# Expert slots with the weights as the stationary operand, fetched slot by slot

## What is computed

```python
# layer 0: 16 experts, hidden width 512, each token goes to its 2 best
h = relu(einsum('bsd,edh->bseh', tensor, W1) + b1)
y = einsum('bseh,ehm->bsem', h, W2) + b2
out = einsum('bse,bsem->bsm', gate, y)
# layer 1: 16 experts, hidden width 176, 2 of them a token, and a shared expert z
a = silu(einsum('td,edh->teh', xf, w1) + b1) * (einsum('td,edh->teh', xf, w3) + b3)
y = einsum('teh,ehd,te->td', a, w2, cw) + cw @ b2
```

## Time and profile before

| | us |
|---|---|
| median of 3 runs (548.8 to 549.23) | 548.93 |
| profiled execution, its own time | 548.54 |
| its span, first to last instruction | 546.8 |
| busy: TensorE, VectorE, ScalarE, GpSimd | 440.9, 364.3, 264.4, 250.2 |
| mean granted TensorE clock, as a share of 2.4 GHz | 0.922 |

### The profile page before, as it was taken

The page is one execution under the profiler, slowest core; times in us unless marked ns, Lnnn a source line. Parts: engine busy times, 40 slices in busy tenths (PEclk is TensorE's granted clock), DMA queues, the critical chain, the costliest instruction groups (busy, mean ns, idle before and its releaser), DMA issues.

```text
span 546.8 us, 10536 instructions
## 1 busy us (share of the span) xinstructions
PE 440.9 (81%) x2430; PEld 303.7 (56%) x2430; DVE 364.3 (67%) x1181; ACT 264.4 (48%) x666; POOL 250.2 (46%) x322
## 2 busy tenths in 40 slices
PE   4889733999999992799889889988657779999950
PEld 3667611777777770256555555545524456777730
DVE  6879940355555552679999999999644445656636
ACT  3357610444444430757777678667232115656520
POOL 3105771143444444336348558457549002656560
PEclk9999755899999996989999999999778999999985
DMA  7999874212122604834122500000003020222107
GB/s 240 348 272 247 243 144 81 55 51 55 47 58 55 223 16 127 205 69 96 38 59 70 132 10 21 0 22 21 15 25 99 19 60 22 78 76 79 49 12 231
DMA packets 63420, 51.52 MB, mean 94 GB/s; under 512 B 9180, under 2 KB 54733, under 8 KB 63234
## 3 DMA queue, kind: packets, MB, share of 16 engines
q1 hardware_dynamic: 56434, 40.86, 29.2%
q0 software_dynamic: 5056, 8.48, 4.6%
q10 hardware_dynamic: 1872, 1.52, 1.2%
HBM read 37.19 MB, written 15.60 MB: 97 GB/s over the span
## 4 chain that ended last, share of the span: by engine, by line
PE 46%; DVE 31%; issue 11%; POOL 4%; DMA 4%; ACT 2%; SPq 0%; DVEq 0%; POOLq 0%; ACTq 0%
PE bank L1505 15%; PE bank L1520 8%; PE bank L1597 4%; PE bank L1513 4%; PE bank L1659 4%; DVE qk_sums L1202 4%; POOL sorted_tokens L716 3%; DVE work L1195 3%; DVE big L1195 3%; DVE work L1239 3%; PE bank L1498 2%; PE bank L1551 2%; DVE ln_stats L258 2%; PE bank L1651 2%; PE bank L1627 2%
## 5 line engine op out<-in xcount | busy, mean ns | idle before, releaser
L725 POOL DMA_INDIRECT results<-work x94 | 91.7, 975 | 139.3 <-DVE work L1172 76.3
L1158 DVE TENSOR_TENSOR work<-bank,bias_big 128x512 f32<-128x512 f32 (+1 forms) x94 | 57.1, 608 | 94.0 <-PE bank L1505 92.5
L857 ACT ACTIVATE work<-bank,mcol 128x128 f32<-128x128 f32 x94 | 43.0, 458 | 115.7 <-PE bank L1498 115.7
L1551 PE MATMUL bank<-late,work 128*128 128x512 f32 x192 | 94.6, 621 | 2.4 <-ACT work L873 2.2
L1505 PE MATMUL bank<-big,work 128*128 x188 | 91.4, 568 | 3.6 <-ACT work L857 3.6
L1551 PEld LDWEIGHTS bank<-late,work 128*128 128x128 f32 x192 | 33.9, 195 | 30.6 <-issue 27.0
L1520 PE MATMUL bank<-big,work 128*128 x376 | 49.7, 275 | 0.0
L1520 PEld LDWEIGHTS bank<-big,work 128*128 128x128 f32 x376 | 45.8, 192 | 0.1
L716 POOL DMA_INDIRECT sorted_tokens<-late,router_at x32 | 31.1, 973 | 27.1 <-DVE late L1107 17.6
L766 POOL DMA_INDIRECT sorted_tokens<-rows,router_at x32 | 31.2, 976 | 13.1 <-issue 7.9
L1505 PEld LDWEIGHTS bank<-big,work 128*128 128x128 f32 x188 | 28.8, 194 | 13.1 <-issue 13.1
(11 more groups left out here) (223 smaller groups left out, 984.5 us busy)
## 6 DMA issues: line engine op xcount, KB each, us to landing
work<-sorted_tokens SPq DMA_DIRECT2D x94, 65.0 KB, 1.8
big<-in_w SPq DMA_DIRECT2D x48, 88.0 KB
big<-in_W SPq DMA_DIRECT2D x1, 4096.0 KB
bias_big<-in_b SPq DMA_DIRECT2D x16, 256.0 KB
big<-results SPq DMA_DIRECT2D x16, 256.0 KB, 3.5
sorted_tokens<-zeros SPq DMA_DIRECT2D x2, 975.0 KB
sorted_tokens<-zeros SPq DMA_DIRECT2D x24, 65.0 KB
late<-in_WqkvbT SPq DMA_DIRECT2D x1, 1544.0 KB
```

The costliest lines, as they stand in the source:

```text
L725: pool.indirect_dma_start(ys[l], bass.IndirectOffsetOnAxis(xg[b][:, D:D + 1].bitcast(I32), 0), yo[b], None, bounds_check=TOPK * T - 1, oob ...
L857: act.activation(xgT[b % 2], bank[:, ends[b % 2], 0:P], ACT.Identity, bias=scale_shift[0], scale=scale_shift[1]).then_inc(e_xTc, 1)
L1158: dve.tensor_tensor(hb[b % 2][:, 0:width], bank[:, 1 + b % 2, 0:width], bias_big[:, bass.ds(e * width, width)], ALU.add).then_inc(e_hb, 1)
L1551: last = pe.matmul(bank[:, 2 * k + i, :], h3T[b], Wqkvb[:, k * HD + i * 512:k * HD + (i + 1) * 512], start=True, stop=True)
```

## The change

- Layer 0: the four 128-column blocks of W1 are now the stationary operands and the 128 turned tokens move. The hidden tile comes out with hidden units on partitions, in two banks. The four transposes are gone. The bias is a column (`b1c`): ScalarE does relu with bias on two blocks, VectorE on the other two.
- Layer 1: w1 and w3 are cut in halves of 88 columns, which are stationary (four products). ScalarE does silu with bias out of PSUM on two halves; VectorE does (second product + bias) * silu in one operation for each half. The two transposes and the copy are gone.
- Stages follow closer on each other (lags of TensorE 0, 1, 2 in place of 0, 1, 2, 3 and 0, 1, 3, 4). ScalarE now looks the expert up too.
- W1, w1 and w3 no longer stand in SBUF. A ring of 8 buffers holds the weights of 8 slots. SyncE fetches them for each slot, after its own look-up: one transfer of 256 KB in layer 0, two of 88 KB in layer 1. The first four slots' weights are issued before the wait for the sorted rows, the others among the row loads. `slot_turn` waits for rows and weights together.
- The broadcast bias loads are gone; the biases are loaded as rows, turned by TensorE once and copied by VectorE before the slots of layer 0.

```diff
+        NW, LEAD = 8, 4
+        w1r = [big[:, H0 * b:H0 * (b + 1)] for b in range(NW)]
-            sp.dma_start(W1s.rearrange("p (e h) -> p e h", e=E), W1.rearrange("e d h -> d e h")).then_inc(ld_w0, 16)
...
-                sp.dma_start(bias_big[:, e * H0:(e + 1) * H0], all_row(b1[e, :], H0)).then_inc(ld_w0, 16)
...
+                def load_expert(t):
+                    if t >= NW:
+                        sp.wait_ge(e_h, l * SLOTS + t - NW + 1)
+                    e = bass.ds(experts(t, 1)[0], 1)
+                    if l == 0:
+                        sp.dma_start(w1r[t % NW].rearrange("p (a h) -> p a h", a=1),
+                                     W1[e, :, :].rearrange("e d h -> d e h")).then_inc(e_x[t % NX], 16)
+                    else:
+                        for k, w in enumerate((w1, w3)):
+                            sp.dma_start(w13r[t % NW][:, k * H1:(k + 1) * H1].rearrange("p (a h) -> p a h", a=1),
+                                         w[e, :, :].rearrange("e d h -> d e h")).then_inc(e_x[t % NX], 16)
...
+                for t in range(LEAD):
+                    load_expert(t)
                 rows_written()
-                run_slots(sp, SLOTS, NX, [(0, None), (0, load)], table(mybir.EngineType.SP, tbl, 0, ROWS - P))
+                for s in range(SLOTS + NW):
+                    if s < SLOTS:
+                        load(s, s % NX, s // NX, place(s, 1)[0])
+                    if LEAD <= s < NW:
+                        load_expert(s)
+                    if s >= 2 * NW:
+                        load_expert(s - NW)
...
+            def slot_hidden(t, b, q, e):
+                pe.wait_ge(e_xTc, t + 1)
+                after(pe, e_hTc, t - 1)
+                after(pe, e_hb, t - 1)
                 for c in range(C0):
-                    last = pe.transpose(bank[:, 3 + b % 2, c * P:(c + 1) * P], hb[b % 2][:, c * P:(c + 1) * P], ident[:, :])
+                    last = pe.matmul(hidden_half(b, c), w1r[t % NW][:, c * P:(c + 1) * P], xgT[b % 2],
+                                     start=True, stop=True)
...
             def silu(t, b, q, e):
+                act.wait_ge(e_h, SLOTS + t + 1)
+                after(act, e_act, t - 1)
+                for c in range(2):
+                    last = act.activation(silu1[b % 2][:, c * P:(c + 1) * P], hidden_part(b, 0, c), ACT.Silu,
+                                          bias=b13c[:, 0, bass.ds(e * 2 + c, 1)])
...
             def gated(t, b, q, e):
                 dve.wait_ge(e_silu, t + 1)
+                after(dve, e_o, SLOTS + t - 1)
+                for c in range(2):
+                    last = dve.scalar_tensor_tensor(hbT[b % 2][0:K1, c * P:(c + 1) * P], hidden_part(b, 1, c),
+                                                    b13c[:, 1, bass.ds(e * 2 + c, 1)],
+                                                    silu1[b % 2][:, c * P:(c + 1) * P], ALU.add, ALU.mult)
```

More of the change, by code:

```diff
@@ L217, in build @@
         xgT = [work[:, 2080 + P * b:2080 + P * b + P] for b in range(2)]
-        hb = [work[:, 2336 + H0 * b:2336 + H0 * (b + 1)] for b in range(2)]
         hbT = [work[:, 3360 + H0 * b:3360 + H0 * (b + 1)] for b in range(2)]
-        act1 = [work[:, 4384 + 176 * b:4384 + 176 * b + H1] for b in range(2)]
+        silu1 = [work[0:K1, 2336 + 2 * P * b:2336 + 2 * P * (b + 1)] for b in range(2)]
         sh_at = ob + 12 * D
@@ L526, in uses, with hidden_half, hidden_part, landed @@
             return len(range(b, SLOTS, NX))
+        def hidden_half(b, c):
+            return bank[:, 1 + 2 * (2 * c // C0) + b % 2, (c % (C0 // 2)) * P:(c % (C0 // 2) + 1) * P]
+        def hidden_part(b, k, c):
+            return bank[0:K1, 1 + 2 * k + b % 2, c * P:(c + 1) * P]
+        LOADS = (32, 48)
+        def landed(l, t):
+            return LOADS[0] * (t // NX) if l == 0 else LOADS[0] * uses(t % NX) + LOADS[1] * (t // NX)
         def moved(l, t):
@@ L861, in relu @@
             def relu(t, b, q, e):
-                act.wait_ge(e_hT, t + 1)
+                act.wait_ge(e_h, t + 1)
                 after(act, e_o, t - 1)
-                act.activation(hbT[b % 2], bank[:, 3 + b % 2, :], ACT.Relu).then_inc(e_hTc, 1)
+                for c in range(C0 // 2):
+                    last = act.activation(hbT[b % 2][:, c * P:(c + 1) * P], hidden_half(b, c), ACT.Relu,
+                                          bias=b1c[:, bass.ds(e * C0 + c, 1)])
+                last.then_inc(e_hTc, 1)
             zero_rows(act, mybir.EngineType.Activation, 0, E // 2, E // 2)
-            run_slots(act, SLOTS, NX, [(0, tokens(0, router0["ss"])), (2, relu)])
+            act.wait_ge(s_mod_ready, 6)
+            run_slots(act, SLOTS, NX, [(0, tokens(0, router0["ss"])), (0, None), (1, relu)],
+                      table(mybir.EngineType.Activation, tbl, P, E - 1))
             def hidden1(t, b, q):
@@ L941, in silu @@
             def silu(t, b, q, e):
[L942 to L951, removed]
+                act.wait_ge(e_h, SLOTS + t + 1)
[3 more added lines that the diff above has]
+                                          bias=b13c[:, 0, bass.ds(e * 2 + c, 1)])
+                last.then_inc(e_silu, 1)
+            act.wait_ge(ld_w1, 32 * E)
+            run_slots(act, SLOTS, NX, [(0, tokens(1, router1["ss"])), (0, None), (1, silu)],
+                      table(mybir.EngineType.Activation, tbl, P, E - 1))
         @block.vector
@@ L1150, in _, with relu_half @@
             slots_as_row(0)
[L1153 to L1160, removed]
+            def relu_half(t, b, q, e):
+                dve.wait_ge(e_h, t + 1)
+                after(dve, e_o, t - 1)
+                for c in range(C0 // 2, C0):
+                    last = dve.tensor_scalar(hbT[b % 2][:, c * P:(c + 1) * P], hidden_half(b, c),
+                                             b1c[:, bass.ds(e * C0 + c, 1)], 0.0, ALU.add, ALU.max)
+                last.then_inc(e_hb, 1)
             def result(t, b, q, e):
@@ L1522, in slot_out @@
                 last.then_inc(e_o, 1)
-            pe.wait_ge(ld_w0, 32 + 32 * E)
-            run_slots(pe, SLOTS, NX, [(1, slot_hidden(0, W1s, H0)), (0, slot_turn(0)), (2, slot_turn_hidden),
-                                      (3, slot_out), (0, None)], experts)
+            pe.wait_ge(ld_w0, 64 + 16 * E)
+            pe.transpose(bank[:, 3, 0:E * C0], b1r[:, :], ident[0:E * C0, 0:E * C0])
+            for k in range(2):
+                last = pe.transpose(bank[0:K1, 3, E * (C0 + 2 * k):E * (C0 + 2 * k + 2)], b13r[:, k, :],
+                                    ident[0:2 * E, 0:2 * E])
+            last.then_inc(s_mod, 1)
+            pe.wait_ge(s_mod_ready, 6)
+            run_slots(pe, SLOTS, NX, [(0, slot_turn(0)), (1, slot_hidden), (2, slot_out), (0, None)], experts)
             pe.wait_ge(e_yo, SLOTS)
@@ L1644, in _, with slot_out1 @@
             pe.wait_ge(t_ready, 2)
[L1647 removed]
+            def slot_out1(t, b, q, e):
                 pe.wait_ge(e_act, t + 1)
[L1649 to L1656 removed]
                 after(pe, e_yo, SLOTS + t - 1)
```

78 lines of the change are left out of this document (38 added, 40 removed).

## The result

The changed kernel takes 563.7 us (median of 4 runs, 561.9 to 564.8) against 549.0 us on the same chip: a ratio of 1.027, 95% interval [1.024, 1.029]. Forecast were 550.5 us and a range to 560. The direction is the forecast one, the size is not: 14.8 us lost in place of 1.6.

What follows compares the result with a forecast made beforehand. TensorE was taken to bound the kernel before; after, TensorE layer 0 and SyncE's issues layer 1. 548.54 - 20.0 (layer 0) + 21.6 (layer 1) = 550.1 us profiled, 550.5 as median; range 541 to 560, own range 547 to 554.

Steps and rivals of the forecast that it cites:

- Layer 0, TensorE: Layer 0's slots: four transposes gone, hidden product 0.89 us; 0.11 + 0.89 + 0.89, about 1.90 us a slot instead of 2.30.
- two charges: Layer 0: 0.7 us (0 to 2) for early fetches beside the last scattered rows, 1.1 us once for slot 8's late weights.
- no queue on GpSimd: Layer 0's end: after slot 46's product no scatters queue, so the last scatter comes at 187.0 instead of 206.94.
- Layer 0, SyncE: Layer 0's fetch queue: row load 0.98 plus weight fetch 0.86 make 1.84 us a slot, just under TensorE's 1.90.
- its 8.5 us: Layer 0's start: from 91.25 to slot 3's hidden product, 9.5 us at half clock, taken as 8.5 for an earlier clock rise.
- the rival of a held layer 0: Fetches also hold layer 0: landings lengthen or SyncE needs 2.05 us a slot; 6 us more, 556, worst about 566; chance 0.18.
- Between the slots: Stretch outside the slots: weight and bias loads leave or shrink, but the chain there runs elsewhere; nothing gained or lost.
- Layer 1, SyncE: Layer 1's queue: row load, wait, look-up and two issues make 2.39 us a slot; last issue ends at 544.6; layer +21.6 us.
- SyncE's slot is 2.2 to 2.3: Rival for layer 1: a cheaper second fetch or free wait shortens SyncE's slot; 543 to 547 us, faster; chance 0.16.
- Layer 1, TensorE: Layer 1 with weights there: work 1.45, hand-over 1.70, two buffers share it, (1.45 + 1.70)/2 = 1.58 us a slot.
- The rival of the clock: Layer 1: TensorE, with 1.45 us of work in 2.39, partly falls to the 1.2 GHz level; +10, 560 us; chance 0.10.
- The Trainium skill's rule on look-ups: Register load floor about 600 ns: both look-ups add 0.65 us a SyncE slot, layer 1 near 3.0, layer 0 near 2.5; no chance.

Runs made afterwards that it cites:

- no_fetch: Changed kernel with all experts' weights resident and slot t taking expert t mod 16, no fetch per slot, output not the reference's; 531.0 us, ratio 0.969.
- lead_1: Changed kernel with one weight fetch ahead of the wait for the sorted rows instead of four, both layers; 562.3 us, ratio 1.024.
- fetch_earlier: Changed kernel with each fetch from slot 8 on queued three row loads earlier on SyncE, both layers; 554.9 us, ratio 1.012.
- look_ups_by_four: Changed kernel with SyncE's look-ups of rows and experts made for four slots at a time; 542.4 us, ratio 0.990.
- after_mended: Changed kernel with look-ups for four slots, fetches queued three row loads earlier, and layer 1's output product one step later; 533.6 us, ratio 0.975.
- one_fetch: Changed kernel with w3's transfer left out in layer 1, one 88 KB fetch a slot, output not the reference's; 544.9 us, ratio 0.994.
- half_bytes: Changed kernel with both of layer 1's fetches cut to 88 of 176 columns, as many issues, output not the reference's; 562.5 us, ratio 1.027.
- no_fetch_out_later: no_fetch with layer 1's output product three steps behind the turn instead of two, output not the reference's; 518.7 us, ratio 0.945.
- one_issue: after_mended with one early fetch, and layer 1's w1 and w3 resident, copied into the ring by one DMA issue a slot; 523.5 us, ratio 0.956.

## Why the prediction was wrong

By its own steps, on the profiled execution (564.8 against 550.1 forecast, 14.7 us; layer 0 accounts for 7.7, layer 1 for 6.3, the stretch between them for 0.4, the end and rounding for the rest).

**Layer 0, TensorE** held: 1.90 us a slot. ScalarE's relu halves are 0.36 us and VectorE's 0.35, as taken; neither wait shows. no_fetch ends layer 0 at 183.7; the forecast without its two charges is 185.2. That this is so near is in part luck. The start was 2.3 us shorter than summed (slot 3's hidden product at 97.45 in no_fetch, forecast 91.25 + 8.5 = 99.75), and the tail 1.0 longer (4.85 us from slot 46's product to the last scatter, forecast 3.8): "no queue on GpSimd" did not hold, the last scatter waits for the one before it.

**Layer 0, SyncE: the two charges failed.** Against no_fetch, the changed kernel loses 11.0 us in layer 0 where I charged 0.7 + 1.1. First the start: 0.7 (0 to 2) for the early fetches, 2.8 measured (first turn 93.03 against 90.24; counted from the table it is 3.6, 14.0 against 10.4). I priced the transfer by its bytes and not by what happens to the small rows that it delays; lead_1 shows it. Second, slot 8: 1.1 charged. The fetch was issued at 108.53, not 106, the wait was 2.6 us, and it did not end there. Timeline of the changed kernel behind it, and the window:

```profile
112.54 1.91 PE L1576 MATMUL bank<-big,work 128*128 x8
114.25 0.42 PE L1549 MATMUL bank<-ident,work 128*128 128x128 f32 x1
...
116.79 0.27 PE L1549 MATMUL bank<-ident,work 128*128 128x128 f32 x1
```

```profile
111.00:115.00 4.00, 3.69 (x21) 3.70 (x22) 0.92 (x4) 1.38 (x4) 0.38 (x1) 0.65 0.72 191
```

The granted clock was 0.65 there, so partly at the 1.2 GHz level, and two slots took 116.79 - 111.31 = 5.5 us instead of 3.8. The stall cost 2.6 + 1.7 = 4.3 us, or 4.4 from slot 7's turn to slot 10's against no_fetch's. Of the other 3.8 us, 0.9 lie before it: the clock rose at 99, 6 us after the first turn, and in no_fetch at 94, 4 us after it. The sum had its 8.5 us for this stretch. The last 2.9 us lie in waits behind slot 10 that the sum did not have at all. The clock has no part in them, it is 1.00 throughout (columns as in the earlier trace rows):

```profile
119.00:190.00 71.00, 69.21 (x613) 68.31 (x612) 45.05 (x144) 38.94 (x108) 34.91 (x37) 1.00 0.74 216
```

Two waits, 0.41 and 1.34 us long, lengthened their slots by 0.6 and 1.5; the other 0.8 is spread over nine slots. The chain of waits of the changed kernel shows how the first came about:

```profile
137.88 3.49 DMA results<-work
...
141.91 0.34 SPq L611
...
142.76 0.35 SPq L619
...
148.34 3.55 DMA big<-in_W
151.94 0.33 PE bank L1549
```

A scatter lands, which frees the buffer for the row load at the head of SyncE's queue; that queue is then worked off at SyncE's own pace (1.86 and 1.88 us a slot here), which leaves next to nothing to catch up with; and the fetch at the end of it needs 3.55 us where a turn is due. The chain of the second, at 168.67, is the same, with a landing of 4.64 us. The prediction compared two periods, 1.84 and 1.90, and not the depth between them: it named "landings lengthen" in the rival of a held layer 0, but not that a fetch stands behind a row load that waits for a scatter. fetch_earlier, which moves the fetch ahead of such loads, and look_ups_by_four, which lets SyncE catch up, each bring 5 to 6 us. Most of that is the stall at slot 8; of the 2.9 us behind slot 10 they leave 1.7 and 2.5 when alone. With both (after_mended) nothing is left: layer 0 takes 93.4 us from its first turn to its last scatter, as in no_fetch (93.5). That rival gave 556 for layer 0 alone held. Its 6 us are near the 7.7 that layer 0 missed, but it had them from a period longer by 0.15 us in 38 slots, and the steady period stayed 1.90: the size is luck.

**Between the slots**: nothing, as forecast (225.2 us against 224.8).

**Layer 1, SyncE** held, and it is the bound: last issue 112.7 us after the table (forecast 112.4), steady period 2.28 (forecast 2.39; the second issue of a pair costs 0.49, not 0.54). one_fetch and half_bytes show that the issue counts: without it layer 1 is 19.9 us shorter, with half the bytes 2.6. By the rival "SyncE's slot is 2.2 to 2.3" the time would have been 543 to 547. The steady period was nearly that, and yet the last issue was no earlier: the queue has irregular gaps, and with them the 29 row loads from 450.90 to 519.88 come 2.38 us apart. So the forecast's 2.39 met the mean by luck: it had no gaps in it, and charged the steady slot 0.11 too much. SyncE's timeline of the changed kernel shows one, 3.24 us from row load to row load:

```profile
464.94 0.34 SPq L611 DMA_DIRECT2D work<-sorted_tokens  x1
...
468.18 0.34 SPq L611 DMA_DIRECT2D work<-sorted_tokens  x1
```

In this gap the pair of fetches takes SyncE 1.68 us in place of 0.82. What holds them up is not known.

**Layer 1, TensorE: the rate of 1.58 failed**, and with it the end. The sum (1.45 + 1.70)/2 took a wait to cost its own length. (Its 0.16 us of waiting for the tokens are an "issue" in the earlier trace rows, a wait without a named cause.) The measured rate without fetches is 1.76: +0.26 on the output product that waits, +0.11 to 0.15 on the turn. My reading is that an instruction that waits also shows its first weight load, which otherwise runs below the instruction before: in no_fetch the output product at 467.67 starts together with its first weight load (467.66), the one at 465.82, which did not wait, 0.11 behind it. no_fetch_out_later shows that the extra time goes with the wait; what it consists of is not shown. At 1.49 (no_fetch_out_later) the work of 1.45 was right. In the changed kernel it meets the last eight slots, where SyncE no longer rules: slot 38's turn at 524.63, 104.3 us after the table (forecast 102.6, its fetch took 3.44 us to land and not 2: +1.7); eight slots to the last turn at 539.91 in 15.3 us and not 12.6 (+2.7); from there to the last scatter 6.9 and not 4.9 (+2.0). Together 6.4, against the 6.3 that layer 1 is off. Not all of the +2.7 is the rate: no_fetch's last eight slots take 14.35 us, and the other 0.9 is the clock, 0.79 from 524 to 532 behind the wait for slot 38's weights. The chain of waits of the changed kernel in these slots:

```profile
534.13 0.71 PE bank L1712 x4
...
535.08 0.92 PE bank L1566 x8
...
537.64 0.15 issue
537.80 0.71 PE bank L1712 x4
```

The hand-over from the product's end at 536.00 to the next output product at 537.80 is 1.80 us, 0.10 more than summed.

**The rival of the clock** was half right. The 0.94 of layer 1's slots (1.00 before) is made of these windows of the changed kernel and of 1.00 in 532 to 540 (columns as in the earlier trace rows):

```profile
449.00:460.00 11.00, 8.11 (x46) 7.65 (x45) 2.50 (x9) 3.84 (x11) 4.05 (x5) 0.71 0.47 122
460.00:524.00 64.00, 44.91 (x352) 39.59 (x350) 22.65 (x84) 29.11 (x81) 25.20 (x26) 1.00 0.49 128
524.00:532.00 8.00, 7.11 (x46) 6.81 (x47) 2.34 (x9) 3.53 (x10) 3.50 (x4) 0.79 0.55 150
```

In the long stretch at SyncE's pace TensorE is busy 44.91 of 64 us and keeps 1.00, against the rival. The clock fell behind two single waits, of 2.26 us at slot 8's turn (451.91) and of 2.12 at slot 38's (524.63), but not behind one of 2.31 at 489.08. After the first, two slots took 2.83 us each, and the next 1.68: SyncE's slack took it up. After the second nothing did, which is the 0.9 us above. In layer 0 it lengthened the slots behind slot 8's stall. The rival looked for neither place.

**The Trainium skill's rule on look-ups** ("DMA: Bandwidth & Descriptors", Latency and other measured facts: a floor of about 600 ns for a register load, spread by unrolling four times) was weighed in the prediction and given no chance. Its figure is not this trace's, 277 ns. Its second half, that unrolling spreads the cost, agrees with look_ups_by_four, where one load brings four values in 302 ns. I had passed it over; it was worth 17.7 us in layer 1.

What would have had to be seen: the range ended at 560 because each rival was priced alone. Layer 0 held (+7.7) and a slower end of layer 1 (+6.3) are not exclusive, and both came. The second was in no rival: the rate of 1.58 stood in the sum without a doubt on it. Slips of addition played no part: 47 row loads at 0.98 are 46.1 and not 46.4, 43 fetches at 1.41 are 60.6 and not 60.5, and the terms behind 547.4 make 552.45 and not 552.3.

What stays open: what the gaps in SyncE's queue are, and why the clock fell behind two of three waits of much the same length. It was not tried to let another engine's queue issue the fetches.

## What to carry to other kernels

Where weights are to stand in the array and the expert is only known at run time, count the issues of the queue that fetches them before anything else: one issue less in a slot was worth 18 us of 564, half the bytes nothing that the measurement can tell. Put a fetch in front of whatever waits in the same queue (9 us here), look up several values at once (21 us), and keep a resident copy if it turns two issues into one (10 us). These gains overlap and don't add up. When a slot has a hand-over just longer than the work that covers it, one more step of lag is worth more than the length of the wait.

## What the runs showed of the hardware

- A register load of four values by SyncE takes 302 ns in the median, one of one value 277 ns, one of eight (from another table) 732 ns.
- An output product of four instructions takes 0.45 us on the chain when it follows without a gap and 0.71 us after a wait for which the chain shows 0.07 to 0.15 us (no_fetch, the changed kernel).
- After 2.6 us without work in layer 0 TensorE's granted clock is 0.65 over the next 4 us. In layer 1 it fell after waits of 2.26 and 2.12 us and stayed at 1.00 after one of 2.31.
- With 1 MB of weight fetches queued, the last scattered rows land after 6.70 us; with 256 KB after 2.56 us, with none after 3.17 (before) and 2.99 (no_fetch).
- A copy of 176 KB inside the on-chip memory lands in 2.1 us in the median (one_issue), the 88 KB fetches from the inputs in 2.0 (changed kernel).
- SyncE spends 0.49 us on a second fetch that follows another without a look-up, the same at 88 KB and at 44 KB a fetch to judge by the slot's 2.28 us.
